# Two hybrid attention and expert layers: epsilon added on GpSimd, and integer expert indices read and written without casts

## The reference

```
def _layernorm(x):
    m = mean(x); v = var(x)
    return (x - m) / sqrt(v + 1e-5)

x = x + attn_a(_layernorm(x))
x = x + ffn(_layernorm(x))
x = x + attn_b(_layernorm(x))
x = x + ffn(_layernorm(x))

def ffn(t):
    logits = t @ Wr.T + br                  # 8 experts
    top_v, top_i = top_k(logits, 2)
    top_w = softmax(top_v)
    router_w = sum(one_hot(top_i, 8) * top_w[..., None], -2)
    o = relu(t @ W1[e].T + b1[e]) @ W2[e].T + b2[e]
    return layer_norm(t + sum over e of o * router_w, gamma, beta)
```

## Time and profile before

| | |
|---|---|
| median of 3 runs | 945.51 us (942.33 to 946.16) |
| profiled execution, its own time | 949.54 us |
| span in it, first to last instruction | 947.7 us |
| PE busy | 791.4 us, 84% |
| DVE busy | 630.8 us, 67% |
| ACT busy | 473.8 us, 50% |
| POOL busy | 434.3 us, 46% |
| chain that ended last | PE 55%, DVE 18%, issue 7%, DMA 7%, SP's queue 5%, ACT 5%, POOL 2% |
| epsilon adds L361 | 65, 235 ns each |
| powers L368 | 65, 793 ns each |
| casts L1066 and L1112 | 32 each, 163 and 164 ns |

### The profile page before, as it was taken

One profiled execution on the slowest core, in us unless ns is written; L12 is line 12 of the kernel. 1 busy time (PEld: TensorE's weight loads), 2 busy tenths in 40 slices (PEclk: granted clock), 3 DMA queues, 4 the chain that ended last, 5 costly groups with the idle time before them and its releaser, 6 DMA issues.

```text
span 947.7 us, 20829 instructions
## 1 busy us (share of the span) xinstructions
PE 791.4 (84%) x6270; PEld 565.3 (60%) x6270; DVE 630.8 (67%) x2348; ACT 473.8 (50%) x1130; POOL 434.3 (46%) x516
## 2 busy tenths in 40 slices
PE   3599989988898899934899998999998799999920
PEld 1356655655687799931455555555544488999920
DVE  3457777764466466644888997898895475666657
ACT  3356666654332233312377776776766432433424
POOL 3002444443466376541243664565322475666643
PEclk9999999996799999975699998999998899999965
DMA  7635554450567777723434534443420378777754
GB/s 198 142 88 122 133 125 121 121 120 28 159 203 222 210 228 240 224 78 105 129 109 132 142 104 123 122 131 108 132 88 27 119 213 251 236 225 240 223 161 123
DMA packets 111668, 142.28 MB, mean 150 GB/s; under 512 B 14912, under 2 KB 90560, under 8 KB 108992
## 3 DMA queue, kind: packets, MB, share of 16 engines
q1 hardware_dynamic: 102480, 122.19, 47.2%
q0 software_dynamic: 9088, 18.89, 5.9%
HBM read 102.89 MB, written 36.66 MB: 147 GB/s over the span
## 4 chain that ended last, share of the span: by engine, by line
PE 55%; DVE 18%; issue 7%; DMA 7%; SPq 5%; ACT 5%; POOL 2%; DVEq 0%; POOLq 0%; ACTq 0%
PE attn L1466 13%; PE attn L740 6%; PE score L1457 6%; PE max L1457 6%; DVE mx L989 6%; PE max L706 5%; PE score L682 4%; PE misc L776 3%; PE misc L748 3%; DMA qst<-scr 2%; PE misc L806 2%; ACT prob L459 2%; PE attn L1446 2%; DMA qst<-mparts 2%; DVE stats L350 1%
## 5 line engine op out<-in xcount | busy, mean ns | idle before, releaser
L989 DVE TENSOR_REDUCE mx<-max 128x2 f32<-128x512 f32 x352 | 237.6, 682 | 83.9 <-PE max L706 77.8
L459 ACT ACTIVATE prob<-score 128x512 f32<-128x512 f32 x352 | 206.1, 602 | 118.0 <-PE score L682 115.3
L1542 POOL DMA_INDIRECT ys<-yt,idw x156 | 150.3, 964 | 113.3 <-DVE yt L1517 85.0
L1289 POOL DMA_INDIRECT xs<-row,index x128 | 127.7, 998 | 149.6 <-ACT prob L459 132.9
L1466 PE MATMUL attn<-wsl,prob 128*128 128x128 f32 x1248 | 157.4, 279 | 2.8 <-DVE prob L1530 2.1
L706 PE MATMUL max<-kst,qst 72*128 72x256 bf16 (+2 forms) x768 | 141.8, 275 | 20.1 <-DVE mx L989 13.3
L1466 PEld LDWEIGHTS attn<-wsl,prob 128*128 128x128 f32 x1248 | 149.0, 195 | 5.7 <-DVE prob L1530 3.7
L682 PE MATMUL score<-qst,kst 74*128 74x256 bf16 (+2 forms) x768 | 138.4, 270 | 3.7 <-DMA qst<-mparts 1.7
L1482 ACT ACTIVATE prob<-score,wsl 128x256 f32<-128x256 f32 x78 | 36.9, 473 | 189.8 <-PE score L1457 189.6
L740 PE MATMUL attn<-prob,vaug 128*32 128x256 f32 (+1 forms) x1536 | 119.8, 385 | 1.0 <-ACT prob L459 0.6
L368 POOL TENSOR_TENSOR rstd<-rstd,halfm 128x2 f32<-128x2 f32 (+1 forms) x65 | 51.5, 793 | 144.6 <-DVE rstd L361 143.6
(11 more groups left out here) (147 smaller groups left out, 1159.2 us busy)
## 6 DMA issues: line engine op xcount, KB each, us to landing
wsl<-in_wall SPq DMA_DIRECT2D x78, 578.0 KB, 4.3
scr<-parts SPq DMA_DIRECT2D x32, 384.0 KB, 3.0
qst<-scr SPq DMA_DIRECT2D x64, 192.0 KB
xt<-xs SPq DMA_DIRECT2D x78, 132.0 KB
kst<-scr SPq DMA_DIRECT2D x16, 576.0 KB
row<-row SPq DMA_DIRECT2D x32, 128.0 KB, 3.9
yg<-ys SPq DMA_DIRECT2D x32, 128.0 KB, 2.9
kst<-scr SPq DMA_DIRECT2D x16, 192.0 KB
```

The source lines that it names most:

```text
L459: nc.scalar.activation(prob[:, g % 2, k, :], pS[(g * NB + k) % 2][:, :], ACT.Exp)\
L989: nc.vector.tensor_reduce(mx[:, sl[4], a:a + 2 * n - 1:2], pM[(g * NB + k) % 2][:, :].rearrange("p (h w) -> p h w", h=n), axis=AX.X, op=AL ...
L1289: nc.gpsimd.indirect_dma_start(out=xs, out_offset=bass.IndirectOffsetOnAxis(ap=index[:, slot, c, k:k + 1], axis=0), in_=row[:, slot, c, k, ...
L1542: nc.gpsimd.indirect_dma_start(out=ys, out_offset=bass.IndirectOffsetOnAxis(ap=idw[:, k, c, 0:1].bitcast(U32), axis=0), in_=yt[:, k, c, :] ...
```

## The change

POOL adds epsilon itself, in front of its power, and waits for its own add; `dve_eps` and its calls are gone from DVE's list (also for TN). The comparison reads the uint32 indices, and the float tile `ixf` and its cast are gone. The reduction over the experts takes the maximum of the products (at most one of the eight is not zero) and writes the uint32 tile `index`; `placed` and its cast are gone. The calls of DVE's list that remain keep their order. The last norm's own epsilon add stays on DVE. Unused semaphores are dropped.

```diff
-        def dve_eps(dve, which, pre, v, slot):
-
-            dve.wait_ge(pre + "_stats", v)
-            nc.vector.tensor_scalar(rstd[:, which, slot, :, 0], mv[:, which, slot, :, 1], EPS, None, ALU.add)\
+        def pool_rstd(pool, which, pre, v, slot):
+
+            pool.wait_ge(pre + "_stats", v, apart=True)
+            nc.gpsimd.tensor_scalar(rstd[:, which, slot, :, 0], mv[:, which, slot, :, 1], EPS, None, ALU.add)\
                 .then_inc(s_(pre + "_eps"), 1)
-
-        def pool_rstd(pool, which, pre, v, slot):
-
             pool.wait_ge(pre + "_eps", v)
             half = halfm[:, which, :] if isinstance(which, slice) else halfm[:, 0, :]
             nc.gpsimd.tensor_tensor(rstd[:, which, slot, :, 1], rstd[:, which, slot, :, 0], half, ALU.pow)\
...
-                    elif i == 2:
-                        dve_eps(dve, which, "n", v, slot)
                     elif NORM in on_:
                         dve_bias(dve, LN, "n", v, slot)
...
                     elif i == 3:
                         dve.wait_ge("ix8_done", v)
-                        nc.vector.tensor_copy(ixf[:, :, :], ix8[:, slot, :, 0:2]).then_inc(s_("ixf_done"), 1)
-                    elif i == 4:
-                        dve.wait_ge("ixf_done", v)
-                        nc.vector.tensor_tensor(oh[:, :, :, :], ixf[:, :, :].unsqueeze(3).to_broadcast([P, QC, 2, E]),
+                        nc.vector.tensor_tensor(oh[:, :, :, :],
+                                                ix8[:, slot, :, 0:2].unsqueeze(3).to_broadcast([P, QC, 2, E]),
                                                 iota8.unsqueeze(1).unsqueeze(1).to_broadcast([P, QC, 2, E]),
                                                 ALU.is_equal).then_inc(s_("oh_done"), 1)
...
                         dve.wait_ge("pick_done", v)
-                        nc.vector.tensor_reduce(placed[:, :, :], pick[:, :, :, :], axis=AX.X, op=ALU.add)\
-                            .then_inc(s_("placed_done"), 1)
-                    else:
-                        dve.wait_ge("placed_done", v)
-                        nc.vector.tensor_copy(index[:, slot, :, :], placed[:, :, :]).then_inc(s_("index_done"), 1)
+                        nc.vector.tensor_reduce(index[:, slot, :, :], pick[:, :, :, :], axis=AX.X, op=ALU.max)\
+                            .then_inc(s_("index_done"), 1)
...
-                        else:
-                            dve_eps(dve, TN, "t", v, slot)
-                    if RTE in on_ and i == 3:
+                    if RTE in on_ and i == 2:
                         dve_bias(dve, TN, "t", V[RTE], sl[RTE])
```

More of the change, by code:

```diff
@@ L211, in build @@
         ix8 = sb("ix8", [P, RING, QC, 8], U32)
-        ixf = sb("ixf", [P, QC, 2])
         oh = sb("oh", [P, QC, 2, E])
@@ L216, in build @@
         pick = sb("pick", [P, QC, 2, E])
-        placed = sb("placed", [P, QC, 2])
         index = sb("index", [P, RING, QC, 2], U32)
@@ L273, in build @@
         for name in """consts_in x_in proj_in weights_in consts_made geo_made filled vaug_zero wq_ps wq_made ones_set spare_in
-            c_sum c_add c_stats1 c_stats c_eps c_rstd c_bias c_norm c_gam c_bet c_x
+            c_add c_norm c_gam c_bet c_x
             n_stats1 n_stats n_eps n_rstd n_bias ln_ready lnT_ps lnT_sb qk_ps part1 less1 part2 less2 part3 v_ps v_sb
@@ L277, in build @@
             pr_ps x_ready t_stats1 t_stats t_eps t_rstd t_bias t_ready tT_ps tT_sb lg_ps lg_done mx8_done ix8_done
-            ixf_done diff e_done oh_done ohb_done den_done w0_done w1_done rank_ps place_done rank_read pick_done
-            placed_done index_done id_done chain chosen_made table_ps tiles_known pad_known pads_in xT_ps xT_sb idw_done h_ps h_act h_dve y_ps
+            diff e_done oh_done ohb_done den_done w0_done w1_done rank_ps place_done rank_read pick_done
+            index_done id_done chain chosen_made table_ps tiles_known pad_known pads_in xT_ps xT_sb idw_done h_ps h_act h_dve y_ps
             ysum_sb xf_done yt_sb out_w flags_set x_bet l_add l_stats1 l_stats l_eps l_rstd l_bias l_norm l_gam
@@ L1143, in t_stats @@
                 def t_stats(i):
-                    if TNS in on_ and i < 3:
+                    if TNS in on_ and i < 2:
                         v, slot = V[TNS], sl[TNS]
@@ L1164, in step @@
                     shift(0)
-                    t_stats(3)
+                    t_stats(2)
                     more(1, 1)
@@ L1172, in step @@
                     more(1, 1)
-                    norms(2)
                     maxima(0, 2)
@@ L1176, in step @@
                     choose(0)
-                    norms(3)
+                    norms(2)
                     maxima(1, 1)
@@ L1181, in step @@
                     more(1, 0)
+                    maxima(1, 2)
                     choose(3)
-                    maxima(1, 2)
                     choose(4)
-                    choose(5)
                     more(1, 0)
@@ L1189, in step @@
                     t_stats(1)
-                    t_stats(2)
                     more(1, 1)
-                    for i in range(5):
+                    for i in range(4):
                         send_to(i)
@@ L1209, in step @@
                     more(1)
-                    t_stats(3)
+                    t_stats(2)
                     maxima(1, 1)
-                    send_to(4)
                     more(2)
@@ L1226, in step @@
                     maxima(2, 3)
+                    maxima(3, 0)
                     choose(3)
+                    maxima(3, 1)
+                    choose(4)
                     norms(2)
[L1229 to L1233, removed]
                     if early(li, s, on_):
```

## The result

After: **934.19 us**, median of 5 runs (931.71 to 938.00), against 945.51 (942.33 to 946.16). The ratio is 0.9869, 95% interval 0.9837 to 0.9902: faster by 1.3%, where 946.4 us (940.0 to 952.0) was forecast. The profiled execution after took 934.19 (span 932.3), that of before 949.54 (947.7): 15.4 us apart, 4 more than the medians, because that execution of before was 4 above its median.

A forecast was written before the change was run, and what follows sets the result against it. The prediction took TensorE (PE) as the main bound, 55% of the chain, against VectorE's 18% and GpSimd's 2%. Its terms, -1.4 - 0.4 + 0.5 + 0.9 + 1.3 = +0.9 us on 945.51, gave 946.4 us, range 940.0 to 952.0.

The forecast's parts named there:

- Sign: Whole kernel: the terms were forecast to sum to +0.9 us, that is slightly slower.
- Rival B: Both attentions: DVE, not PE, is the floor and every slot removed pays; -8.4 us, 937.1 us, chance 0.16.
- Index cast, "-1.4 us": First attention: removing DVE's cast at L1112 saves 0.10 us in each of 14 rounds, -1.4 us.
- Shorten by over 0.15: First attention: rounds shortening by over 0.15 us would mean the exponential did not cover the epsilon add.
- Hidden epsilon add in the first attention: First attention: the add hides behind DVE's wait for ScalarE's exponential, so moving it gains nothing there.
- cast to float at 0: L1066 on DVE: removal gains nothing in the first attention or steady second attention, where DVE waits behind it.
- POOL's add: Ahead of POOL's power: add 0.19, own wait 0.08, statistics wait 0.11; scatter to bias 0.38 us longer.
- the 0.11 for the new wait: POOL, ahead of the power: waiting on the statistics was priced at 0.11 us more.
- Steady rounds, "+0.1 each": Five second-attention rounds with the long add: 0.38 us delay, PE absorbs only 0.29; +0.1 each, +0.5 us.
- Three rounds, "+0.3 each": Rounds at 475, 490, 579: bias follows the power closely, no long add behind; +0.3 each, +0.9 us.
- Exposed norms, "+0.14": Nine norms for which POOL stands idle: statistics to power grows from 0.29 to 0.43; +0.14 each, +1.3 us.

The follow-up runs named there:

- casts_only: Kernel before with both casts removed and the epsilon add left on DVE; ratio 0.9917 to before.
- castout_only: Kernel before with only the index cast removed, the reduction writing the integer index; ratio 0.9961 to before.
- eps_only: Kernel before with only the epsilon add moved from DVE to POOL, both casts kept; ratio 0.9973 to before.
- castin_only: Kernel before with only the cast of the indices to float removed, the comparison reading integers; ratio 1.0000 to before.
- after_two_adds: Kernel after with POOL adding half of epsilon twice, so one more add and wait; ratio 0.9949 to before.
- before_again: Kernel before, unchanged, run again on an experiment chip for a second profile; ratio 0.9969 to before.
- after_again: Kernel after, unchanged, run again on the same chip for a second profile; ratio 0.9886 to before.
- before_shift64: Kernel before with 64 small padding writes on DVE ahead of the second attention's loop; ratio 0.9974 to before.
- after_shift78: Kernel after with 78 small padding writes on DVE ahead of the second attention's loop, putting its end at 1627; ratio 0.9959 to before.

## Why the prediction was wrong

- **Sign.** I forecast +0.9 us; the medians say -11.3. Rival B named 937.1, but by luck: DVE is not the floor. The second attention's round shortened by 0.08, not to under 17.4, and the first attention owes nothing to the epsilon add.
- **Index cast, "-1.4 us".** Right place, wrong size. I took the cast's distance to its successor, 0.10, from the earlier trace rows and left out its distance from its predecessor. From reduction to maxima it is 0.32 before and 0.10 after, and casts_only and castout_only give 0.21 a round: -2.9 us if all 14 rounds gave it; eight are shown to. "Shorten by over 0.15" was to prove the exponential no cover; it did not, for eps_only left the round at 12.52. That test mixed up two causes.
- **Hidden epsilon add in the first attention, cast to float at 0.** Both confirmed (eps_only, castin_only).
- **POOL's add.** 0.24 us where I took 0.19, and 0.08 to the power as priced; the 0.11 for the new wait did not appear. Scatter to bias grew by 0.31, not 0.38.
- **Steady rounds, "+0.1 each".** The bias waits for the power, the ranks are late, the queries close up: all as forecast, and after_two_adds bears the mechanism out. But I read one of PE's two gaps (0.29) and missed 0.11 behind it: 0.31 - 0.40 = -0.09, measured -0.08.
- **Three rounds, "+0.3 each".** The one at 579 is the round of the loop's end: without the stop it takes 17.64 with epsilon on DVE (casts_only) and 17.93 with it on POOL, +0.29. The stop buried this. The rounds at 475 and 490 lie in the uneven stretch, and no run isolates them.
- **Exposed norms, "+0.14".** At the start of the second attention the statistics end at 414.55 after and the power starts at 414.96: 0.41 where it was 0.29, so +0.12. Timeline of POOL after:

```profile
414.64 0.23 POOL L359 TENSOR_SCALAR rstd<-mv 128x4 f32<-128x4 f32 x1 [3.13 <-DVE mv L353]
414.96 1.03 POOL L363 TENSOR_TENSOR rstd<-rstd,halfm 128x4 f32<-128x4 f32 x1
```

- **The step that failed most was not in the sum.** The round of 22.03 us, with 2.40 of idle time that nothing in the program explains, stood in the trace that I had read. I took rounds beside it and never asked why it was 4.4 longer, nor what fewer DVE instructions ahead of it would do. It is 4.1 of the profiles' 15.4 us. With the measured sizes in the sum's own terms it would have come to about -1.7 (-2.9 - 0.4 - 0.4 + 0.9 + 1.1, an estimate that keeps the terms no run isolates), so the index cast alone turned the sign, and the term put at nothing is more than twice that.
- **Not settled.** Start-up (1.66), the expert tiles (2.97) and what the casts leave of the seven mixed rounds (4.41 less some 1.3) vary between kernels that hardly differ there, and the second pair of profiles lacks the last two: the seven rounds took 103.75 us in before_again, 103.82 in after_again, 109.63 in castin_only and 112.79 in before_shift64, whose padding comes later. I count them as not due to the change. That leaves 2.9 + 4.1 = 7.0 us with a cause that runs show, of 11.3 in the medians; the 0.4 of the second attention's other rounds has none. Of the 7.0, castout_only shows the first part in time (0.9961, near the edge of noise) and casts_only the sum (0.9917), while no median shows the second part by itself. The remaining 4 us of the medians are unexplained; profiles of kernels that do the same work lie further apart (spans of 961.8 in before_again and 974.5 in before_shift64). Why the same loop stops or not by its place has an answer that fits, below, but the fetch itself was not seen.

## What to carry to other kernels

Price an instruction that goes by the time from its predecessor's start to its successor's, with and without it; if it reads what its predecessor wrote, that wait goes too. Before you forecast an edit to an engine's list, look for rounds longer than their neighbours and for idle time put down to "issue", above all behind a loop's branch: such a stop depended here on where the code lies, an edit anywhere ahead of it moved it, and padding shows in one profile whether a round's gain is the edit's or the place's; whether it reaches the median takes many executions. When a delayed chain shortens a round, add up all the gaps of the engine that bounds it, not only the first.

## What the hardware showed unexpectedly

- DVE stood still for 2.3 to 3.3 us behind the branch that closes the loop of the second attention, with the loop's end at instruction 1610, 1627 or 1628, and not at 1549 to 1609 or 1691. The Trainium skill, Runtime: NRT & Kernel Launch, "Instruction fetch mechanics", says that most engines hold two blocks of 256 instructions and that a taken branch to a place outside them waits for a fetch. The trace agrees: the loop has 277 to 289 instructions between its two branches, so by place it lies in two such blocks or in three. Put one block's border between 1609 and 1610, where the pair of single casts puts it, and the border before lies 256 lower, between 1353 and 1354, an estimate from the page's figure. The loops that stop, and only they, begin before the lower border and end behind the upper one: they begin near 1324, 1338, 1339 and 1350, while those of after, eps_only, casts_only and castin_only end at 1609 or before and that of before_shift64 begins near 1402. The fetch itself was not seen, and one border is fitted, not known.
- A stop of 2.4 us on DVE made its round 4.1 to 4.4 us longer (the longer stops of castout_only and after_shift78 5.1 and 6.1), since PE's granted clock then stood at 0.50 for 6.8 us (584.1 to 590.9): at half clock that is 3.4 us at most, an estimate, and the rest is the stop itself. In after_two_adds the clock fell for as long without a stop, and the round took 2.8 more than its neighbours.
- A two-input add of 128x2 on DVE took 0.65 us while POOL issued a scatter that had 0.6 us to run, in five rounds, and ended with it each time to 0.01 us; one of 128x4 took 0.15 under another scatter (554.46). The Trainium skill, SBUF — State Buffer, "Who interferes with whom", makes two-input DVE instructions contend only with POOL instructions that read SBUF, and infers that issuing a transfer is not one. The trace agrees on `pick`, which lasted until POOL's `r<-yg` was done (0.73 at 556.87); the five long adds speak against the inference and the short ones for it, so it stays open here. The scatter reads its places from the tile `index`, which may matter.
- An add of 128x2 and one of 128x4 on POOL both take 0.22 to 0.26 us, and the power of the same sizes about 0.72 and 1.05.
